# Layer one's kernel product in four row tiles over four banks, new places in its queue, and filler products at the end of retention

## The chip, the cores and the metric

One Trainium2 chip, one of its cores. The metric is the device time of one execution of the whole program in microseconds. Engines: TensorE (PE; PEld is its loading of weights), VectorE (DVE), ScalarE (ACT), GpSimd (POOL), and SyncE (SP), which issues DMAs.

## The reference, cut to what matters

Two layers on x of shape 16 x 1024 x 256. Layer zero is a retention block with an MLP, then a mixture of 16 experts with a top-k choice over all tokens. Layer one is a dynamic convolution with a softmax over 31 taps, then an MLP with a ReLU. The change touches the convolution's kernel and, in layer zero, only what TensorE does while the last tile of retention is normalised.

```python
# layer one, attention: b=16, l=1024, H=16 heads of d=16 channels, K=31 taps
avg = jnp.cumsum(x, axis=1) / jnp.arange(1, l + 1)[None, :, None]
ci = avg.reshape(b, l, H, d).transpose(0, 2, 1, 3).reshape(b * H, l, d)
pc = ci @ W_pe + b_pe                      # the kernel product, 62 columns a head
dyn, gate = pc[..., :K], pc[..., K:]
energy = stt + sigmoid(gate) * dyn         # tanh form: (1 + tanh(gate/2)) * dyn/2
w = softmax(energy, axis=-1)
out = sum over kk of w[:, :, kk:kk+1] * padded[:, kk:kk+l, :]
v = layernorm(out @ W_fc.T + residual) * gamma + beta
# layer one, MLP
h = relu(h4 @ W1 + b1);  y = h @ W2 + b2
```

## The kernel before, in words

All engines run the same list of steps, each its own part of each step, in order. Layer one works on one batch (1024 tokens) at a time, cut in eight chunks of 128 tokens and two halves of 512. The list is made by hand: each step has a place in slots, sixteen slots to a batch (`PLACES_D`; `STARTS_D` for batches 0 and 1), and `order_d` and `layer_one_tiles` sort all steps of all batches by place. Steps of neighbouring batches overlap: a place above 16 falls into the next batch's time. So a place says only what comes before what in each engine's queue; nothing waits for a time. Engines meet through semaphores.

The steps on TensorE in layer one: `turn_in` (eight transposes of 128x128), `kernel_product` (one a chunk), `window_turn` (two transposes), `convolve` (32 matmul records; eleven a batch, of 96 tokens), `mix` (one a chunk), `turn_mid` (eight transposes a half), `l1_expand` and `l1_contract` (eight of each a half, six and twelve matmuls). In one slot stand one `l1_expand` and one `l1_contract`.

PSUM has eight banks. Banks 6 and 7 hold the MLP's sums. `timed_banks` shares out banks 0 to 5 to the other steps in order of place, by a hold time in slots for each kind of step (`BANKS_D`). A bank that is used again is waited for with the semaphore of whoever read it last: a kernel product's banks with `gated_energy` (VectorE, L2318), a convolution's with `convT` (ScalarE, L2215), turn_mid's with `l1_h_full` (ScalarE, L2225), a mix's with `l1_u` (VectorE, L2351), an expansion's with `l1_hidden_low` (VectorE, L2380).

The kernel product of a chunk, before: the 256 channels are two blocks (j) of 128; each block is cut in two row halves of 64 partitions (r), four heads each. A bias product (L2424) of 64 rows and 496 columns opens one bank for each r, then for each j and r a product of 64 rows and 248 columns (L2429) is added. An fp32 matmul shows as two records, the bias (fp32r) as one. Then ScalarE takes the tanh of the gate half of both banks (L2187), VectorE makes the gated energy from the other half (L2318), GpSimd adds the energies of the reference (L2147), VectorE subtracts the maximum (L2324, L2326), ScalarE exponentiates, VectorE divides, SyncE writes the weights to a band in DRAM and loads it back for the convolution.

After retention's last tile the program goes on with the experts' choice: 32 rounds of a search, each a count on VectorE and ScalarE, summed by TensorE (L1703, L1705, L1707); between them stand `turn_logits` in rounds 1 to 4 (four transposes each) and from round 5 on three filler products of 128x256 (`keep_clock`, L1695). Ahead of it the last tile's transposes (L1050) and routing (L1057) wait for a chain of small VectorE, GpSimd and ScalarE instructions.

Of the kernel before, what the change touches and what calls it, by code (L numbers as in the profile page):

```python
# [22 lines left out]
P = 128  # L23
BANK = 512
# [12 lines left out]
    "tensor": ["mod_product0", "cols_turned0"] + [f"mod_product{n}" for n in range(1, 6)] + ["cols_turned1"]  # L37
    + [event for n in range(1, ROUNDS + 1) for event in (f"counted_all{n}", *([f"logits_turned{n - 1}"] if n <= 4 else []))] + ["limits_spread", "first_counted_all", "first_summed", "all_counted", "ties_summed", "rows_summed"]
# [329 lines left out]
def timed_banks(steps, wanted, of, paired=()):  # L368

    free, at = {bank: 0.0 for bank in of}, {}  # L370
# [564 lines left out]
def retention_tensor(K, t, t0, pe):  # L935
# [108 lines left out]
    for h in range(2):  # L1044
        pe.wait_ge(s("xn"), t.N + h)
        bank = take(t.bank["turn_out", i, h], "xnT", KD * i + h + 1)
# [6 lines left out]
    for h in range(2):  # L1053
# [5 lines left out]
        m.then_inc(s("lg_product"), 1)  # L1059

# [619 lines left out]
def expert_tensor(K, t, pe):  # L1680
# [16 lines left out]
    for n in range(1, ROUNDS + 1):  # L1697
# [121 lines left out]
    "l1_split": 0.6, "l1_low": 1.03, "l1_contract": 2.59, "share": (4.65, 12.15), "load": (0.54, 8.56), "join": (4.76, 13.01),  # L1819
    "add_in": (6.08, 13.95), "stats_in": (6.42, 14.39), "root_in": (7.3, 15.44), "norm_in": (7.84, 15.72), "load_bias_row": 4.42,  # L1820
    "turn_in": (9, 17.63), "average": (9.98, 10.16, 17.95, 18.16), "add_row": (11.69, 19.69),
    "kernel_product": (10.8, 12.8, 14.85, 16.8, 18.8, 20.8, 22.79, 24.8), "gated": (10.8, 12.8, 14.61, 16.8, 18.82, 20.8, 22.8, 24.8),
    "energies": (11.61, 13.56, 15.61, 17.61, 19.47, 21.61, 23.61, 24.94), "exponentials": (11.89, 13.82, 15.85, 17.92, 19.85, 21.85, 23.85, 25.7),
# [817 lines left out]
```

## Time and profile before

| | us |
|---|---|
| median of 3 runs | 3453.86 (3453.41 to 3455.07) |
| profiled execution | 3465.23 |
| its span | 3463.4 |
| TensorE busy in the span | 3306.8 (95%) |
| VectorE busy | 2606.7 (75%) |
| ScalarE busy | 2073.9 (60%) |
| GpSimd busy | 1256.2 (36%) |
| TensorE's mean granted clock | 0.978 |

The busy time is the share in which at least one instruction of the engine ran; matmuls overlap, and their ends are modelled. Retention takes the span to about 1070 us, the experts to about 1940, layer one the rest.

### The profile page before, as it was taken

The page shows a single profiled execution, that of the slowest core. Times are in us where ns is not written, and L with a number is a line of the kernel's source. Part 1 is how long each engine was busy: PE and PEld are TensorE (multiplying, and loading weights), DVE is VectorE, ACT ScalarE, POOL GpSimd, SP SyncE. Part 2 cuts the span into 40 slices and gives each one's busy share as a digit, 9 for nine tenths or more (in the row PEclk, how much of TensorE's full clock was granted, in tenths as well). Part 3 has the DMA queues.
Part 4 walks back from the last instruction along what each step waited for, and adds up shares of the span by engine and source line. Part 5 has one row for each costly group of instructions (what it writes and reads, how often), then busy time and mean ns, then how long its engine had stood idle before and what let it go on. Part 6 is the DMA issues. An engine that isn't in the chain of part 4 may idle for free.

```text
span 3463.4 us, 67571 instructions
## 1 busy us (share of the span) xinstructions
PE 3306.8 (95%) x25145; PEld 2791.9 (81%) x25145; DVE 2606.7 (75%) x6178; ACT 2073.9 (60%) x4056; POOL 1256.2 (36%) x1076
## 2 busy tenths in 40 slices
PE   7999999999997899999999469999999999999999
PEld 4888888888886789999999448888888888888888
DVE  5877887788878865555554588888888888888884
ACT  4677777777665455556665345555555555555554
POOL 1333323333322256656655332333333332322320
PEclk8999999999998999999999779999999999999999
DMA  5332233222212544444444365555555555655541
GB/s 180 102 115 99 84 114 108 82 66 76 75 45 80 93 103 106 95 106 106 107 95 91 84 132 117 117 121 126 129 125 127 121 123 126 130 126 127 128 102 41
DMA packets 746054, 366.38 MB, mean 106 GB/s; under 512 B 551311, under 2 KB 696279, under 8 KB 745591
## 3 DMA queue, kind: packets, MB, share of 16 engines
q1 hardware_dynamic: 717246, 319.55, 36.9%
q0 software_dynamic: 28416, 42.49, 6.9%
q8 instruction: 201, 3.29, 0.4%
q14 instruction: 127, 1.03, 0.1%
q10 hardware_dynamic: 64, 0.02, 0.0%
HBM read 224.93 MB, written 135.99 MB: 104 GB/s over the span
## 4 chain that ended last, share of the span: by engine, by line
PE 88%; DVE 6%; ACT 2%; issue 1%; DMA 1%; SPq 1%; POOL 1%; another core or an unknown queue 0%; ACTq 0%; DVEq 0%; POOLq 0%
PE bank L2479 11%; PE bank L2493 10%; PE bank L1015 10%; PE bank L1781 10%; PE bank L1797 10%; PE bank L994 10%; PE bank L2450 7%; PE bank L130 5%; PE bank L971 3%; PE bank L2429 3%; PE bank L2461 3%; PE bank L2424 1%; ACT sides L1327 1%; PE bank L979 1%; PE bank L1007 1%
## 5 line engine op out<-in xcount | busy, mean ns | idle before, releaser
L1670 DVE TENSOR_TENSOR hidden_low<-bank,hidden_high 128x512 fp32r<-128x512 f32 x256 | 176.2, 689 | 247.3 <-ACT hidden_high L1380 148.9
L641 ACT ACTIVATE bank<-bank,b 128x512 f32<-128x512 f32 x256 | 172.4, 673 | 281.5 <-PE bank L994 281.2
L1373 ACT ACTIVATE bank<-bank,fc_bias 128x512 f32<-128x512 f32 x256 | 169.6, 663 | 253.5 <-PE bank L1781 231.9
L1015 PE MATMUL bank<-w_high,gT_low 128*128 128x256 f32 x1024 | 309.6, 302 | 2.9 <-DVE gT_low L782 2.9
L2237 ACT ACTIVATE bank<-bank,l_b 128x512 f32<-128x512 f32 x256 | 168.8, 659 | 239.4 <-PE bank L2479 239.4
L2493 PE MATMUL bank<-l_w_high,l_hidden_low 128*128 128x256 f32 x1024 | 307.5, 300 | 0.0
L2450 PE MATMUL bank<-bandT,window 128*32 128x96 f32 x5632 | 272.7, 345 | 22.4 <-DMA bandT<-bands 18.9
L1015 PE MATMUL bank<-w_high,gT_high 128*128 128x256 f32 x1024 | 289.5, 283 | 0.0
L1015 PE MATMUL bank<-w_low,gT_high 128*128 128x256 f32 x1024 | 289.4, 283 | 0.0
L2493 PE MATMUL bank<-l_w_low,l_hidden_high 128*128 128x256 f32 x1024 | 285.9, 279 | 0.0
L2493 PE MATMUL bank<-l_w_high,l_hidden_high 128*128 128x256 f32 x1024 | 285.6, 279 | 0.0
L2450 PEld LDWEIGHTS bank<-bandT,window 128*32 128x32 f32 x5632 | 194.7, 123 | 84.7 <-issue 48.1
L782 DVE TENSOR_TENSOR gT_low<-bank,gT_high 128x512 fp32r<-128x512 f32 x256 | 173.0, 686 | 112.5 <-ACT gT_high L648 112.5
L2147 POOL TENSOR_TENSOR energies<-energies,energy 128x496 f32<-128x496 f32 x128 | 161.7, 1264 | 207.6 <-DVE energies L2318 207.6
L1293 POOL DMA_INDIRECT moe_output<-ys,idx x128 | 204.1, 1594 | 70.4 <-issue 55.1
L2479 PE MATMUL bank<-h4T_high,l_w_low 128*128 128x512 f32 x512 | 222.9, 435 | 6.7 <-DVE l_v L2351 6.7
L1015 PEld LDWEIGHTS bank<-w_high,gT_low 128*128 128x128 f32 x1024 | 195.1, 191 | 24.0 <-issue 13.1
L2493 PEld LDWEIGHTS bank<-l_w_high,l_hidden_low 128*128 128x128 f32 x1024 | 192.6, 188 | 23.4 <-issue 19.0
L994 PE MATMUL bank<-hT_high,w_low 128*128 128x512 f32 x512 | 203.7, 398 | 2.7 <-POOL hT_low L563 2.7
L1015 PEld LDWEIGHTS bank<-w_low,gT_high 128*128 128x128 f32 x1024 | 195.4, 191 | 12.0 <-issue 7.2
L994 PE MATMUL bank<-hT_low,w_high 128*128 128x512 f32 x512 | 203.4, 397 | 0.0
L2479 PE MATMUL bank<-h4T_high,l_w_high 128*128 128x512 f32 x512 | 202.8, 396 | 0.0
(400 smaller groups left out, 10703.7 us busy)
## 6 DMA issues: line engine op xcount, KB each, us to landing
bandT<-bands SPq DMA_DIRECT2D x352, 240.0 KB, 3.7
fc_full<-in_L_ffn_fc_wT SPq DMA_DIRECT2D x32, 1024.0 KB
bands<-zeros SPq DMA_DIRECT2D x22, 768.0 KB, 8.6
x<-in_L_attn_x SPq DMA_DIRECT2D x32, 512.0 KB, 6.3
moe_output<-zeros SPq DMA_DIRECT2D x32, 512.0 KB, 7.2
moe<-moe_output SPq DMA_DIRECT2D x32, 512.0 KB, 7.0
x_after_retention<-x SPq DMA_DIRECT2D x31, 512.0 KB, 2.8
moe_input_and_gates<-xn SPq DMA_DIRECT2D x31, 512.0 KB, 7.8
```

Of the source, the lines that this page charges most:

```text
L130: t = pe.transpose(bank[:, i * rows:(i + 1) * rows], source(i), ident[0:rows, 0:rows])
L641: e.activation(bank[:, :], bank[:, :], ACT.Gelu_apprx_tanh, bias=t.b1[:, f:f + 1]).then_inc(s("g_full"), 1)
L782: v.tensor_tensor(t.gT.low[:, f % SLICES, :], K.banks[t.bank["expand", i, f, 0]][:, :], t.gT.high[:, f % SLICES, :], ALU.subtract).then_in ...
L994: m = pe.matmul(bank[:, :], w, h, start=k + j == 0, stop=k == KD - 1 and j == 2)
L1015: m = pe.matmul(out, x, w, start=False, stop=f == KF - 1 and j == 2 and c % 2 == 1)
L1293: e.indirect_dma_start(K.moe_dram, bass.IndirectOffsetOnAxis(ap=t.idx[i % 4][:, n:n + 1], axis=0), t.ys[i % 2][:, n, :], None, compute_op= ...
L1670: v.tensor_tensor(t.hidden.low[:, n % SLICES, :], K.banks[t.bank["expand", i, f, 0]][:, :], t.hidden.high[:, n % SLICES, :], ALU.subtract) ...
L1781: m = pe.matmul(bank[:, :], w, y, start=k + j == 0, stop=k == KD - 1 and j == 2)
L1797: p = pe.matmul(y_chunk(K, ch), y, w, start=first and j == 0, stop=f == KF - 1 and j == 2 and ch % 2 == 1)
L2450: m = pe.matmul(bank[32 * g:32 * (g + 1), k * TT:(k + 1) * TT], t.window[n % 2][:, pair, odd, :], t.bandT[n % 2][:, :, g // 2 * H // 2 + k ...
L2479: m = pe.matmul(bank[:, :], w, x, start=k + j == 0, stop=k == KD - 1 and j == 2)
L2493: p = pe.matmul(K.banks[6 + ch // 2][:, left:left + D], x, w, start=False, stop=f == KF - 1 and j == 2 and ch % 2 == 1)
```

## The change

Layer one. The kernel product is cut in four row tiles of 32 partitions (two heads of each block), each into a bank of its own: four bias products of 248 columns, then for each block four products of 124 columns, where there were two of 496 and two of 248 for each block. The order of heads in the energies follows, and so do the constants made on the host, the loads (14 instead of 10) and the view that tanh and gated energy read (four banks of 124 elements, 496 in all as before). A kernel product takes the banks 0 to 3, all four; expansions take only 4 and 5; all other steps 0 to 3. All places are new.

Retention. Twenty-four filler products of 128x256 (fp32, so two records each) are put on TensorE between the last contraction of the last tile and its transposes, in groups of 5, 5, 6, 5 and 3, the later four each behind a wait. Three of the four `turn_logits` move from rounds 1 to 3 of the search to the end of retention, with five fillers behind them; the fourth moves to round 1, and rounds 2 to 4 get fillers.

```diff
 def timed_banks(steps, wanted, of, paired=(), homes={}):
+        home = homes.get(name, of)
         if name in paired:
-            first = min(of[::2], key=lambda b: max(free[b], free[b + 1]))
-            taken = [first, first + 1]
+            first = min(home[:len(home) - number + 1], key=lambda b: (max(free[b:b + number]), -sum(free[b:b + number])))
+            taken = list(range(first, first + number))
         else:
-            taken = sorted(of, key=lambda b: free[b])[:number]
+            taken = sorted(home, key=lambda b: free[b])[:number]
...
 def retention_tensor
+    halves = [take(t.bank["turn_out", i, h], "xnT", KD * i + h + 1) for h in range(2)]
+    def keep_clock(count):
+        for _ in range(count):
+            pe.matmul(halves[1][:, 0:D], K.ident[:, :], t.w_ret[:, 0, :], start=True, stop=True)
+    keep_clock(5)
+    for signal, value, count in (("x1", t.N, 5), ("x1", t.N + 1, 6), ("h2", t.N, 5), ("var_rms", t.N, 3)):
+        pe.wait_ge(s(signal), value)
+        keep_clock(count)
...
+    pe.wait_ge(s("centered"), t.N)
+    for n in range(3):
+        turn_columns(pe, K.banks[4 + n], C, lambda c: K.logits[:, (n * C + c) * P:(n * C + c + 1) * P], K.ident, s("tensor_setup"))
+    keep_clock(5)
...
 def expert_tensor
-        if n <= CH // PER_BANK:
-            turn_logits(n - 1)
+        if n == 1:
+            turn_logits(CH // PER_BANK - 1)
         else:
             keep_clock(3 if n < ROUNDS else 1, 2 * P)
...
-    "kernel_product": (10.8, 12.8, 14.85, 16.8, 18.8, 20.8, 22.79, 24.8),
+    "kernel_product": (11.07, 12.98, 14.92, 16.69, 18.96, 20.99, 22.77, 24.6),
-    "convolve": (16.82, 18.13, 19.59, 21.03, 22.48, 23.93, 25.38, 26.83, 28.28, 29.73, 31.18),
+    "convolve": (16.8, 18.08, 19.67, 21.36, 22.28, 23.89, 25.49, 26.84, 28.19, 29.73, 31.09),
-    "turn_mid": (29.71, 36.62),
+    "turn_mid": (30.8, 37.6),
...
 BANKS_D = {
-    "turn_in": (2, 0.44), "kernel_product": (2, 0.7), "window_turn": (1, 0.48), "convolve": (1, 0.45), "mix": (1, 0.61), "turn_mid": (2, 0.18),
-    "l1_expand": (1, 1.97),
+    "turn_in": (2, 0.77), "kernel_product": (4, 0.37), "window_turn": (1, 0.55), "convolve": (1, 0.46), "mix": (1, 2.41),
+    "turn_mid": (2, 1.48), "l1_expand": (1, 2.27),
 }
+HOMES_D = {name: range(4) for name in BANKS_D} | {"l1_expand": range(4, 6)}
...
-            for r in range(2):
-                rows = slice(r * P // 2, (r + 1) * P // 2)
-                pe.matmul(pair[r][:, 0:4 * t.RW], t.ones[rows, :], t.pe_bias[rows, :, :, :, :].rearrange("o a j q k -> o (a j q k)"), start=True, stop=False)
+            for r in range(t.NR):
+                rows = slice(r * P // t.NR, (r + 1) * P // t.NR)
+                pe.matmul(pair[r][:, 0:2 * KD * t.RW], t.ones[rows, :], t.pe_bias[rows, :, :, :, :].rearrange("o a j q k -> o (a j q k)"), start=True, stop=False)
             for j in range(KD):
-                for r in range(2):
-                    rows = slice(r * P // 2, (r + 1) * P // 2)
+                for r in range(t.NR):
+                    rows = slice(r * P // t.NR, (r + 1) * P // t.NR)
```

The expansion's place is unchanged, 33.2 and then every slot; the contraction's moves from 2.59 to 2.53 slots behind it. In the queue of a steady batch after the change, `window_turn` 10 stands at 30.54, a contraction at 30.73, `turn_mid` of half 0 at 30.8, the next batch's `kernel_product` 2 at 30.92 (14.92), `convolve` 10 at 31.09, `mix` 6 at 31.11, an expansion at 31.2.

## Rows read from the trace of the kernel before

**Rows 1.** The page, part 1: busy time, share of the span, instructions.
```profile
PE 3306.8 (95%) x25145; PEld 2791.9 (81%) x25145; DVE 2606.7 (75%) x6178; ACT 2073.9 (60%) x4056; POOL 1256.2 (36%) x1076
```

**Rows 2.** Windows: busy us of each engine, granted clock, DMA share, GB/s.
```profile
1080.00:1090.00 10.00, 8.84 (x33) 7.36 (x31) 7.68 (x25) 6.09 (x13) 0.00 (x0) 0.62 0.71 255
1090.00:1100.00 10.00, 8.53 (x45) 7.09 (x44) 9.82 (x32) 7.23 (x16) 1.04 (x1) 1.00 0.18 59
2480.00:2570.00 90.00, 89.52 (x828) 73.95 (x827) 77.91 (x159) 52.30 (x106) 27.44 (x22) 1.00 0.57 125
```

**Rows 3.** Waits from 2100 to 3400 us: total us, times, longest.
```profile
DVE top L2324 <- POOL energies L2147: 87.9, 84, 2.0
...
PE bank L2479 <- DVE l_v L2351: 6.7, 14, 0.5
```

**Rows 4.** Timeline of TensorE in two batches: start us, us, engine, line.
```profile
2479.99 0.49 PE L2424 MATMUL bank<-pe_bias,l_ones 64*128 64x496 f32 x2
...
2570.00 0.49 PE L2424 MATMUL bank<-pe_bias,l_ones 64*128 64x496 f32 x2
...
2602.86 0.49 PE L2424 MATMUL bank<-pe_bias,l_ones 64*128 64x496 f32 x2
2603.18 1.00 PE L2429 MATMUL bank<-w_pe,avgT 64*128 64x248 f32 x8
2604.11 1.56 PE L2450 MATMUL bank<-bandT,window 128*32 128x96 f32 x32
...
2607.32 1.04 PE L130 MATMUL bank<-ident,moe 128*128 128x128 f32 x8
```

**Rows 5.** Timeline around one kernel product with idle readers.
```profile
2491.97 0.49 PE L2424 MATMUL bank<-pe_bias,l_ones 64*128 64x496 f32 x2
...
2493.34 0.58 ACT L2187 ACTIVATE l_th<-bank 128x496 f32<-128x496 f32 x1 [0.20 <-PE bank L2429]
...
2493.96 0.67 DVE L2318 SCALAR_TENSOR_TENSOR energies<-l_th,bank 128x496 f32<-128x496 f32 x1 [0.34 <-ACT l_th L2187]
```

**Rows 6.** Timeline around one turn_mid.
```profile
2444.38 1.04 PE L130 MATMUL bank<-ident,l_v 128*128 128x128 f32 x8
...
2445.01 1.45 ACT L2225 ACTIVATE l_h_full<-bank,mod_columns 128x512 f32<-128x512 f32 x2 [0.65 <-PE bank L130]
2446.35 1.14 ACT L2231 CAST h4T_high<-l_h_full 128x512 fp32r<-128x512 f32 x2
```

**Rows 7.** Timeline around one convolution.
```profile
2609.69 1.50 PE L2450 MATMUL bank<-bandT,window 128*32 128x96 f32 x32
...
2611.11 0.50 PE L2479 MATMUL bank<-h4T_high,l_w_low 128*128 128x512 f32 x1
...
2611.25 0.32 ACT L2215 COPY convT<-bank 128x192 f32<-128x192 f32 x1 [0.65 <-PE bank L2450]
```

**Rows 8.** Timeline of TensorE at the end of retention and in the search.
```profile
1063.41 2.19 PE L1050 MATMUL bank<-ident,xn 128*128 128x128 f32 x8 [9.76 <-DVE xn L890]
...
1074.35 0.35 PE L1707 MATMUL bank<-count,ones_of_count 128*128 128x2 f32 x1
...
1087.71 0.25 PE L1707 MATMUL bank<-count,ones_of_count 128*128 128x2 f32 x1
...
1089.87 0.25 PE L1707 MATMUL bank<-count,ones_of_count 128*128 128x2 f32 x1
...
1089.98 1.54 PE L1695 MATMUL bank<-logits,block_ones 128*128 128x256 f32 x6
```

**Rows 9.** Timeline: an expansion, the draining of its bank, the next but one.
```profile
2572.72 0.50 PE L2479 MATMUL bank<-h4T_high,l_w_low 128*128 128x512 f32 x1
...
2574.22 0.38 PE L130 MATMUL bank<-ident,avgT 128*128 128x128 f32 x2
...
2582.93 0.67 DVE L2380 TENSOR_TENSOR l_hidden_low<-bank,l_hidden_high 128x512 fp32r<-128x512 f32 x1
...
2583.40 0.48 PE L2479 MATMUL bank<-h4T_high,l_w_low 128*128 128x512 f32 x1
```

More of the change, by code:

```diff
@@ L1043, in retention_tensor @@
     i, q = t.N - 1, P // C
-    for h in range(2):
+    halves = [take(t.bank["turn_out", i, h], "xnT", KD * i + h + 1) for h in range(2)]
[6 more added lines that the diff above has]
+        keep_clock(count)
+    for h, bank in enumerate(halves):
         pe.wait_ge(s("xn"), t.N + h)
-        bank = take(t.bank["turn_out", i, h], "xnT", KD * i + h + 1)
         for k in range(KD):
@@ L1818 @@
 PLACES_D = {
[L1819 to L1822, printed above, removed]
@@ new lines @@
+    "norm_in": (8.66, 14.98), "load_bias_row": 3.83, "turn_in": (9.17, 16.89), "average": (9.5, 9.63, 16.92, 18.28),
+    "add_row": (11.84, 19.96), "kernel_product": (11.07, 12.98, 14.92, 16.69, 18.96, 20.99, 22.77, 24.6),
+    "gated": (10.93, 12.74, 14.76, 16.64, 18.55, 20.58, 22.76, 24.59),
+    "energies": (11.31, 13.55, 15.76, 17.45, 19.29, 21.42, 23.52, 25.44),
+    "exponentials": (12.04, 14.05, 15.81, 18.0, 20.12, 22.01, 23.98, 25.68),
+    "softmax": (12.53, 14.65, 16.56, 18.43, 20.63, 22.63, 24.33, 26.31),
@@ L1830 @@
+    "turn_mid": (30.8, 37.6), "load_out_row": 38.29, "gain_out": (42.51, 50.94), "result": (47.78, 57.02),
 }
@@ L1945, in layer_one_tiles @@
     t.x2, t.moe = K.ring(ctx, "x2_", 2, [P, HC, D]) + more_x2, K.ring(ctx, "moe", 2, [P, HC, D])
-    t.loads = 16 * 10
+    t.loads = 16 * 14
     course = sorted(((2 * KF * b + place, n, name, b, *args) for b in range(K.B) for n, (place, name, *args) in enumerate(order_d(KF, b))), key=lambda z: z[:2])
     t.steps = [(name, b, *args) for _, _, name, b, *args in course]
-    t.bank = timed_banks([(time, *step) for time, _, *step in course], BANKS_D, range(6), ("kernel_product",))
+    t.bank = timed_banks([(time, *step) for time, _, *step in course], BANKS_D, range(6), ("kernel_product",), HOMES_D)
     t.pieces, t.w_count, sent = {}, {}, [0, 0]
@@ L1996, in layer_one_sync @@
     loads = [(t.out_full[0:2, :, :], A["L1_ffn_b2"].rearrange("(a b d) -> a b d", a=1, b=1).to_broadcast([2, 2, D]))]
-    loads += [(t.pe_full[r:r + 2, :, :, :, :].rearrange("o a j q k -> o (a j q k)"), A["pe_bias_row"].to_broadcast([2, 4 * t.RW])) for r in (0, P // 2)]
+    loads += [(t.pe_full[r:r + 2, :, :, :, :].rearrange("o a j q k -> o (a j q k)"), A["pe_bias_row"].to_broadcast([2, 2 * K.KD * t.RW])) for r in range(0, P, P // t.NR)]
     def load_half(b, half):
@@ L2249, in kernel_view @@
     first = t.bank["kernel_product", b, ch, 0]
-    assert t.bank["kernel_product", b, ch, 1] == first + 1
-    two = K.psum[:, first * BANK:(first + 2) * BANK].rearrange("p (r c) -> p r c", r=2)
-    return two[:, :, part * K.KD * t.RW:(part + 1) * K.KD * t.RW]
+    assert all(t.bank["kernel_product", b, ch, r] == first + r for r in range(t.NR))
+    tiles = K.psum[:, first * BANK:(first + t.NR) * BANK].rearrange("p (r c) -> p r c", r=t.NR)
+    return tiles[:, :, part * K.KD * t.RW:(part + 1) * K.KD * t.RW]
 def layer_one_vector(K, t, v, c):
```

110 lines of the change are left out of this document (58 added, 52 removed).

## The prediction, made before the changed kernel ran

> **What bounds the kernel now.** I read the page first: TensorE is busy for 3306.8 us, 95% of the span [rows 1]. That counts overlapping matmuls with modelled ends, so it names the engine and no more. The windows come next. A steady batch of layer one holds 89.52 us of TensorE work in 90 us at a granted clock of 1.00, against 77.9 us of VectorE, 52.3 of ScalarE and 27.4 of GpSimd [rows 2]. The first kernel product of one batch starts at 2479.99 and that of the next at 2570.00, so a batch takes 90.0 us [rows 4]. The view of waits between 2100 and 3400 us has one wait of TensorE, 14 times 0.48 us: an expansion whose bank VectorE hasn't yet drained of a mix [rows 3]. VectorE's own longest wait there is 87.9 us for GpSimd's sum of the energies [rows 3]. So in layer one TensorE's issue order is the path and the rest fits beneath it, VectorE with the least room (12 us in 90, much of it spent in waits). Fourteen batches, 2 to 15, run so. Batches 0 and 1 are a start-up paced by other engines and by DMA.
>
> The second place is the end of retention. The granted clock is 0.62 for 1080 to 1090 us and 1.00 in the ten after [rows 2], behind an idle stretch of 9.76 us in which TensorE waits for the last normalised tile [rows 8]. Those hundred microseconds are a chain through VectorE, ScalarE and TensorE, so the lost clock lies on the path.
>
> **Part A, TensorE kept busy at retention's end.** The count of a search round starts at 1074.35 (round 2), 1087.71 (round 7), 1089.87 (round 8): five rounds at the low clock took 13.36 us, one at the full clock 2.16 [rows 8]. At 2.16 the five take 10.8, which is 2.6 us less. Against it stand 24 added filler products of 128x256 ahead of the last tile, two records each. Six such records have their first start at 1089.98 and end 1.54 us later [rows 8], so with 0.28 for one record's run they start 0.25 apart at most; I take 0.22, 0.43 us a product and 10.4 us for 24. The last work before the idle stretch ends at 1053.65 (1063.41 less 9.76), so they run to about 1064, 0.6 us past the 1063.41 at which the first transposes start now; those then take half as long, and the second half waits for VectorE as before. After the routing, twelve transposes at 0.11 and five fillers come to 3.5 us. With the routing half as long they end near 1070.3. The next stage begins about then anyway: its second count is at 1074.35, its first a slow round earlier. If they are 1 us late, Part A is worth 1.6. I take **2.6 us**, between 0 (the clock isn't held) and 3.5 (round 1 and the routing gain too).
>
> **Part B, the kernel product.** Now two bias products of 496 columns, then eight records of 248 on 64 rows: 2602.86 to 2604.11, 1.25 us [rows 4]. The eight take 1.00 us from the first start to the last end; the two halves of the array run side by side (eight one after another at the 0.207 us that 496 column passes need at 2.4 GHz would take 1.66). So there are four steps of 0.207 us. The change makes four tiles of 32 rows: sixteen records of 124 columns, still four steps if four tiles run side by side. A step is then no longer set by its columns (0.103) but by loading 128 columns of weights: eight transposes with such loads and few columns take 1.04 us including one run of 0.27 [rows 4], so 0.11 us a step. The four steps fall from 0.83 to 0.44, the bias phase by half of 0.207. A product takes 0.75 us, **0.50 less; eight a batch, 4.0 us.** Tanh and the gated energy keep their 496 elements.
>
> The bounds: no gain would need the four tiles to run in pairs, 0 us. Between them lies what the convolution shows, the only tiles cut four ways in this trace: 32 records in 1.56 us with runs near 0.34 [rows 4], 0.157 us for a step of four tiles whose 192 column passes need 0.08. If row tiles keep such a step, four take 0.63 and the product 0.95: 2.4 us a batch. I take 0.11, since here, unlike in the convolution, the trace shows row tiles whose loads hide (eight records in 1.00 us).
>
> The Trainium skill, "TensorE: Matmul & The Clock Gate", section "Measured speedup vs the span model", has 3.07 times for four row tiles of 512 columns, not four. By that, as an estimate, a step of 0.11 becomes 0.14 us, the product gains 0.37 us, and the forecast would be some 15 us later. No run here shows it yet.
>
> **What the four banks cost.** Each kernel product now takes banks 0 to 3 at once. It can't start until all four are drained, and nothing but an expansion (banks 4, 5) or a contraction (6, 7) can run until VectorE has finished the gated energy. From an undisturbed product: start 2491.97, tanh 2493.34, gated 2493.96 to 2494.63 [rows 5]. The banks are free 2.66 us after the start, with the shorter product 2.16, so 1.4 after its end. An expansion or a contraction is about 1.5 us (expansion 2572.72, next step 2574.22 [rows 9]), which just covers it. Sorting the new places of a steady batch gives the queue. Products 3, 4, 5, 6, 7 have one such step behind them, products 0 and 1 two: covered. Product 2 has none: its places run turn_mid 14.80, kernel_product 14.92, convolve 15.09.
>
> - Product 2. turn_mid uses banks 2 and 3. In the trace its transposes start at 2444.38, ScalarE's copies at 2445.01 for 1.45, its casts at 2446.35 for 1.14 [rows 6]. Banks are free 2.1 us after the start, so the product starts there and not at 0.95; its tanh, third in ScalarE's queue, starts at about 3.0; tanh and gated energy end 1.3 us later; the convolution starts at 4.4. With no waits it would start at 1.75. **2.65 us** a batch.
> - Product 0 stands right behind a convolution. Convolution 2609.69, copy 2611.25 for 0.32, TensorE's next step now 2611.11 [rows 7]: **0.5 us**.
> - Products 3 and 7: an expansion is just ahead, so its ReLU is ahead of the tanh, and VectorE is short of time there by the sum of its instructions. I take **0.3 us each**, between nothing and one 0.67 us VectorE instruction.
>
> That is 3.75 us a batch. The wait of 0.48 us goes, as expansions have banks of their own. Net: 4.0 + 0.48 - 3.75 = 0.7 us a batch, **10 us** in fourteen. In batches 0 and 1 products wait for averages and bands; four small DMAs more at the start lie under the load that layer one waits for. I put both at nothing, give or take 4.
>
> The Trainium skill's page "TensorEngine Tiling (Array Packing)", sections "PSUM Bottleneck" and "Gotcha 1: PSUM Pressure", warns of just this: row tiles need a bank each, and draining doesn't get faster. The trace agrees that draining takes longer (1.4 us after the product) than the product itself (0.75).
>
> **Sum.** 10 + 2.6 = 12.6 us. The profiled execution took 3465.2 us (span 3463.4), 11 above the median of the runs, so I take off the difference only: 3453.9 - 12.6, about **3441 us**.
>
> **Rivals.**
> 1. *The order hides the waits.* If ScalarE reaches product 2's tanh early, or what waits there is made up by work TensorE would have lost elsewhere, most of the 4.5 us a batch stays: 14 x 4.5 + 2.6 = 66 us, 3388. For it: VectorE has 12 us spare, and other work now stands between gated and energies. Against it: both engines take steps in order, and turn_mid, tanh and gated energy are one chain.
> 2. *Small tiles don't overlap load and run.* Step 0.157 in place of 0.11: product 0.95, 1.6 us a batch lost, net -0.9: 14 x 0.9 - 2.6 = 10 us slower, 3464. It decides from a step of 0.13 us on. For it the convolution; against it the present row tiles.
> 3. *Two banks for expansions.* Now the expansion started at 2572.72 is drained when VectorE's instruction of 2582.93 ends, 10.9 us later, while the next but one starts at 2583.40 [rows 9]; with two banks it would wait 0.2 us, and TensorE is to be faster. If four of sixteen expansions wait 0.8 us, 3.2 a batch: 45 us lost, 3486. It decides from 0.7 us a batch. Against it: gated energies that must be done at once keep VectorE near TensorE.
> 4. *It washes out:* a microsecond a batch more of waits than I counted, 3450 to 3457.
>
> **Chances.** My sum 0.35, rival 1 0.25, rival 4 0.17, rival 2 0.11, rival 3 0.10, others 0.02. Within 0.2% (7 us) can't be told from no change in this kernel. Rival 1 and most of my case lie below 3447: faster 0.58; same 0.18; slower 0.24. The range for 8 in 10 is 3400 to 3474: it holds my case, 2 and 4 and the nearer part of 1; the far ends of 1 and 3 are left out. My case's own range is 3430 to 3450.
>
> **What would show it.** A kernel product's start to the next step's 0.75 us, and its four records at one time starting within nanoseconds; if it is 0.95, rival 2. The distance of batches 89.3; TensorE idle before the convolution behind product 2 with the gated energy named as releaser, near 2.6 us each time; if it is absent, rival 1. Waits of expansions for hidden_low: rival 3. At retention's end clock 1.00 from 1050 on and rounds of 2.16 from the first; if the clock falls all the same, Part A fails. The forecast is most easily wrong in product 2's wait and in what I left at nothing in batches 0 and 1.

## The result, and the profile after

Median of 13 runs 3463.24 us after, 3455.07 before (13 runs on the same chip). The ratio is 1.0022, 95% interval 1.0014 to 1.0030: 7.6 us slower (4.8 to 10.4). I had forecast 12.6 us faster. The time lies within the range that I gave, on the other side of no change. One of the 13 runs after took 5254 us at a mean granted clock of 0.56; the ratio leaves it out.

The two profiled executions differ by 0.8 us only (3465.2 and 3466.0; spans 3463.4 and 3464.2): that of before lay 10 above its median, that of after 3. The counts of the search end at 1158.47 before, and layer one's first tanh starts 803.5 us later; in the kernel with retention's edit alone, whose code between these points is the same, it is 794.8 us, and 791.7 in the profiled execution after. So that of before lost some ten microseconds there with the same code, and whole spans can't be compared here. Below I compare distances within a stage, and the timed runs.

The busy times of the page:

```profile
PE 3270.6 (94%) x26501; PEld 2773.9 (80%) x26501; DVE 2638.1 (76%) x6178; ACT 2084.1 (60%) x4056; POOL 1304.5 (38%) x1076
```

TensorE is busy 36 us less than in [rows 1], in 1356 more instructions; VectorE 31 us more. The windows (us, busy time of PE, PEld, DVE, ACT, POOL, granted clock, DMA share, GB/s):

```profile
1080.00:1090.00 10.00, 8.89 (x43) 7.31 (x42) 9.15 (x27) 7.71 (x17) 0.00 (x0) 0.93 0.64 241
...
2207.00:2297.00 90.00, 86.62 (x925) 71.93 (x917) 79.75 (x160) 53.13 (x106) 29.25 (x22) 1.00 0.61 126
2476.00:2566.00 90.00, 86.56 (x882) 71.88 (x882) 78.73 (x156) 52.93 (x106) 29.71 (x22) 0.98 0.59 124
```

At retention's end the clock is 0.93 where [rows 2] had 0.62. In layer one TensorE idles 3.4 us of 90, where it idled 0.5; and the third line has a clock of 0.98, where [rows 2] had 1.00 in a batch. The waits from 2100 to 3400 us (total us, times, longest):

```profile
PE bank L2476 <- DVE energies L2344: 21.1, 14, 1.6
...
PE bank L2450 <- ACT l_h_full L2251: 15.5, 13, 1.2
...
DVE top L2350 <- POOL energies L2173: 9.5, 16, 0.8
...
PE bank L2450 <- ACT convT L2241: 8.9, 14, 0.7
...
PEld bank L2505 <- DVE l_hidden_low L2406: 4.3, 14, 0.3
```

The one wait of TensorE in [rows 3] is gone, and three larger ones stand in its place: a convolution for a gated energy, a kernel product for turn_mid's copies, a kernel product for a convolution's copy. A timeline of TensorE, with five starts of batches and, at 2395.94, one product and the step behind it (start, duration, engine, line):

```profile
2206.62 0.39 PE L2450 MATMUL bank<-pe_bias,l_ones 32*128 32x248 f32 x4 [0.64 <-ACT convT L2241]
...
2296.28 0.39 PE L2450 MATMUL bank<-pe_bias,l_ones 32*128 32x248 f32 x4 [0.64 <-ACT convT L2241]
...
2395.94 0.39 PE L2450 MATMUL bank<-pe_bias,l_ones 32*128 32x248 f32 x4
2396.16 0.61 PE L2455 MATMUL bank<-w_pe,avgT 32*128 32x124 f32 x16
2396.70 0.50 PE L2505 MATMUL bank<-h4T_high,l_w_low 128*128 128x512 f32 x1
...
2658.17 0.39 PE L2450 MATMUL bank<-pe_bias,l_ones 32*128 32x248 f32 x4 [0.64 <-ACT convT L2241]
...
2749.33 0.39 PE L2450 MATMUL bank<-pe_bias,l_ones 32*128 32x248 f32 x4 [0.64 <-ACT convT L2241]
...
2839.10 0.39 PE L2450 MATMUL bank<-pe_bias,l_ones 32*128 32x248 f32 x4 [0.64 <-ACT convT L2241]
```

A product takes 0.76 us to the next step's start (1.25 in [rows 4]): as forecast. These batches take 89.66, 91.16 and 89.77 us. Of the thirteen from batch 2 (2115.49) to batch 15 (3292.11) six take 91.1 to 91.3, five 89.7 to 89.8, two 90.2 and 90.7; the last seven alternate. The mean is 90.51, where it was 90.0 and I had forecast 89.3. What makes a long one shows at product 2. All engines there:

```profile
2676.61 1.04 PE L130 MATMUL bank<-ident,l_v 128*128 128x128 f32 x8
...
2677.25 1.45 ACT L2251 ACTIVATE l_h_full<-bank,mod_columns 128x512 f32<-128x512 f32 x2 [0.65 <-PE bank L130]
...
2678.84 0.39 PE L2450 MATMUL bank<-pe_bias,l_ones 32*128 32x248 f32 x4 [1.19 <-ACT l_h_full L2251]
...
2679.73 0.58 ACT L2213 ACTIVATE l_th<-bank 128x496 f32<-128x496 f32 x1
...
2680.35 0.67 DVE L2344 SCALAR_TENSOR_TENSOR energies<-l_th,bank 128x496 f32<-128x496 f32 x1 [1.72 <-ACT l_th L2213]
2680.93 2.35 DVE L2401 TENSOR_TENSOR h4T_low<-l_h_full,h4T_high 128x512 fp32r<-128x512 f32 x2
2681.09 1.64 POOL L2173 TENSOR_TENSOR energies<-energies,energy 128x496 f32<-128x496 f32 x1 [3.51 <-DVE energies L2344]
...
2681.16 1.50 PE L2476 MATMUL bank<-bandT,window 128*32 128x96 f32 x32 [1.50 <-DVE energies L2344]
```

From transposes to product 2.23 us, from product to convolution 2.32, as worked out (2.1 and 2.3). What I had left out comes behind it. The windows of 1 us there, with the clock as the third number from the end:

```profile
2680.00:2681.00 1.00, 0.00 (x0) 0.00 (x0) 0.65 (x2) 1.00 (x3) 0.00 (x0) 1.00 0.80 86
...
2682.00:2683.00 1.00, 1.00 (x19) 0.71 (x11) 1.00 (x1) 0.54 (x2) 0.74 (x1) 0.58 0.79 81
2683.00:2684.00 1.00, 1.00 (x5) 0.81 (x4) 0.89 (x2) 0.00 (x0) 0.00 (x0) 0.50 0.37 50
2684.00:2685.00 1.00, 1.00 (x4) 0.81 (x3) 0.00 (x0) 0.00 (x0) 0.00 (x0) 0.50 0.29 91
2685.00:2686.00 1.00, 1.00 (x4) 0.79 (x4) 0.90 (x3) 0.00 (x0) 0.00 (x0) 0.71 0.55 167
```

After the two idle stretches of 1.19 and 1.50 us the granted clock goes from 1.00 (2.4 GHz) to 0.50 (1.2 GHz) for 3 us, while a mix and an expansion run. The batches of 91.2 us have this, those of 89.7 don't, though they have the same two waits: it happens eight times in the fourteen steady batches. In the batch that starts at 2568.0 the low clock fell in part on the idle stretch itself, and the batch took 90.2.

Retention's end:

```profile
1067.00 1.10 PE L1060 MATMUL bank<-ident,xn 128*128 128x128 f32 x8
...
1074.38 0.27 PE L1724 MATMUL bank<-count,ones_of_count 128*128 128x2 f32 x1 [0.46 <-DVE hits L1461]
...
1088.41 0.25 PE L1724 MATMUL bank<-count,ones_of_count 128*128 128x2 f32 x1
```

The eight transposes take 1.10 us, not the 2.19 of [rows 8]. These counts are of rounds 1 and 7: six rounds in 14.03 us, while before rounds 2 to 7 alone, five, took 13.36 [rows 8]. The last tile came 3 us later in this execution than in that of before, ahead of anything changed. From retention's last product with both high halves (L1016) to the last count of the search it is 104.5 us after (1054.02 to 1158.53), and 107.4 before (1051.06 to 1158.47).

### The profile page after: what moved, and what is told of

Read it like the earlier page. It is cut to its first block, busy times and chain, and to the rows that moved or that the text cites. A ratio compares the mean times of both kernels' runs of the same rounds, so it can differ in the third digit from the quotient of the medians.

```text
span 3464.2 us, 70416 instructions
## 1 busy us (share of the span) xinstructions
PE 3270.6 (94%) x26501; PEld 2773.9 (80%) x26501; DVE 2638.1 (76%) x6178; ACT 2084.1 (60%) x4056; POOL 1304.5 (38%) x1076
## 4 chain that ended last, share of the span: by engine, by line
PE 88%; DVE 4%; ACT 3%; issue 2%; DMA 1%; POOL 1%; SPq 1%; PEldq 0%; PEld 0%; ACTq 0%; POOLq 0%; DVEq 0%
PE bank L2505 11%; PE bank L2519 11%; PE bank L1016 10%; PE bank L1814 10%; PE bank L1798 10%; PE bank L995 10%; PE bank L2476 7%; PE bank L130 6%; PE bank L2487 3%; PE bank L972 3%; PE bank L2455 1%; PE bank L2450 1%; PE bank L2485 1%; ACT sides L1344 1%; PE bank L980 1%
## 5 line engine op out<-in xcount | busy, mean ns | idle before, releaser
L2173 POOL TENSOR_TENSOR energies<-energies,energy 128x496 f32<-128x496 f32 x128 | 195.2, 1525 | 742.1 <-DVE energies L2344 742.1
L1016 PE MATMUL bank<-w_high,gT_low 128*128 128x256 f32 x1024 | 309.6, 302 | 2.9 <-DVE gT_low L783 2.9
L2476 PE MATMUL bank<-bandT,window 128*32 128x96 f32 x5632 | 264.0, 340 | 36.8 <-DVE energies L2344 27.1
L1016 PE MATMUL bank<-w_high,gT_high 128*128 128x256 f32 x1024 | 289.5, 283 | 0.0
L1016 PE MATMUL bank<-w_low,gT_high 128*128 128x256 f32 x1024 | 289.4, 283 | 0.0
L2476 PEld LDWEIGHTS bank<-bandT,window 128*32 128x32 f32 x5632 | 188.1, 123 | 91.5 <-issue 64.4
L1310 POOL DMA_INDIRECT moe_output<-ys,idx x128 | 212.2, 1658 | 70.4 <-issue 55.1
L2505 PE MATMUL bank<-h4T_high,l_w_low 128*128 128x512 f32 x512 | 230.2, 450 | 0.1
L1016 PEld LDWEIGHTS bank<-w_high,gT_low 128*128 128x128 f32 x1024 | 195.1, 191 | 24.0 <-issue 13.1
L1016 PEld LDWEIGHTS bank<-w_low,gT_high 128*128 128x128 f32 x1024 | 195.4, 191 | 12.0 <-issue 7.2
L2505 PE MATMUL bank<-h4T_low,l_w_high 128*128 128x512 f32 x512 | 203.1, 397 | 0.0
```

What stands on the lines that cost most here:

```text
L1016: m = pe.matmul(out, x, w, start=False, stop=f == KF - 1 and j == 2 and c % 2 == 1)
L1310: e.indirect_dma_start(K.moe_dram, bass.IndirectOffsetOnAxis(ap=t.idx[i % 4][:, n:n + 1], axis=0), t.ys[i % 2][:, n, :], None, compute_op= ...
L2173: e.tensor_tensor(e1[:, :, :], e1[:, :, :], t.energy[:, :, :], ALU.add).then_inc(s("full_energy"), 1)
L2476: m = pe.matmul(bank[32 * g:32 * (g + 1), k * TT:(k + 1) * TT], t.window[n % 2][:, pair, odd, :], t.bandT[n % 2][:, :, g * H // t.NR + k * ...
L2505: m = pe.matmul(bank[:, :], w, x, start=k + j == 0, stop=k == KD - 1 and j == 2)
```

## The experiments

**Theory 1:** layer one's steady batches lose the time, by the waits at product 2 and the clock that falls behind them. **Theory 2:** the loss comes from the edit at retention's end. **Theory 3:** VectorE is so full that a wait taken away comes back elsewhere. Theory 4 came up on the way. All kernels were timed against the kernel before on the same chip; the times below are the ratio less one times 3455 us, with the 95% interval. Edits of places are to the steady batches' table alone.

### One part at a time

Retention's end alone: the kernel before with these edits of the change, `keep_clock` groups, `turn_logits` and all.

```diff
+    keep_clock(5)
+    for signal, value, count in (("x1", t.N, 5), ("x1", t.N + 1, 6), ("h2", t.N, 5), ("var_rms", t.N, 3)):
...
-        if n <= CH // PER_BANK:
-            turn_logits(n - 1)
+        if n == 1:
+            turn_logits(CH // PER_BANK - 1)
```

> The kernel before with the edit at retention's end alone (filler products, early turning of three groups of logits); layer one as before. Theory 1 (the loss of 8 us comes from layer one's steady batches: TensorE waits 1.2 us ahead of and 1.5 us behind kernel product 2, and in every second batch the granted clock then falls to one half for some 3 us, 1.5 us more): 2.2 us faster than before, by the lead that the changed kernel's count of round 7 has gained on that of before since the last tile's store of it began. Theory 2 (the loss comes from the edit at retention's end, whose fillers and turned logits delay something that the profile of one execution hides): 3 us or more slower than before.

**Measured:** 5.2 us faster (1.7 to 8.3 faster). The stretch from the last high product to the last count is 105.0 us (107.4 before).

Layer one alone: the changed kernel with these edits taken back.

> The changed kernel with retention's end as before; layer one as changed. Theory 1: the changed kernel's time plus 2.2 us, so 10 us slower than the kernel before. Theory 2: at most the time of the kernel before.

**Measured:** 11.1 us slower than before (7.9 to 14.5); that stretch is 107.6 us. Theory 2 falls. Retention's end brings 2.4 to 3.1 us in the profiles; the timed runs (5.2, and 11.1 less 7.6) agree within their intervals. The loss is in layer one.

### The clock

Filler products in the two waits around product 2, so that these stay and TensorE works in them; four and six, then two and three.

```diff
+            if ch == 2 and b >= 2:
+                for _ in range(4):
+                    pe.matmul(pair[0][:, 0:D], K.ident[:, :], t.w_fc[:, 0, :], start=True, stop=True)
...
+                for _ in range(6):
+                    pe.matmul(K.banks[bank][:, 0:D], K.ident[:, :], t.w_fc[:, 0, :], start=True, stop=True)
```

> The changed kernel with filler products on TensorE in the two waits around product 2, in batches 2 to 15: four products of 128x256 into the product's first bank ahead of it, six into the next expansion's bank behind it. The waits stay, the engine works in them. Theory 1: granted clock 1.00 in all steady batches, which all take 89.7 us in place of 89.7 and 91.2 in turn, so some 10 us less than the changed kernel (3453). If the clock has no part in the loss: the same time as the changed kernel, or up to 3 us more for fillers that run over.

**Measured:** 23.2 us slower than before (18.3 to 27.6). The clock was 1.00 in all steady batches, but they took 91.4 us: the four fillers took 1.8 us and the six 2.8, longer than the waits. The number of fillers was wrong.

> As the run with filler products in the two waits around product 2, but two ahead and three behind in place of four and six. In that run each filler took 0.46 us in place of the 0.22 reckoned with, four took 1.8 us in a wait of 1.2 and six 2.8 in one of 1.5; the granted clock was 1.00 throughout, and batches took 91.4 us, 1.8 more than the 89.6 of the changed kernel's batches at full clock. Theory 1: clock 1.00 in all steady batches, all of 89.7 us, 10 us less than the changed kernel, so within 3 us of before. If the batches of 91.2 had another cause than the clock: 90.5 on average as in the changed kernel.

**Measured:** 0.3 us slower than before (2.8 faster to 3.5 slower), 7.3 less than the changed kernel. A batch, and two starts 89.65 apart:

```profile
2570.00:2660.00 90.00, 88.97 (x918) 73.34 (x916) 80.34 (x159) 52.95 (x106) 30.11 (x23) 1.00 0.59 125
```

```profile
2206.40 0.39 PE L2454 MATMUL bank<-pe_bias,l_ones 32*128 32x248 f32 x4 [0.64 <-ACT convT L2241]
...
2296.05 0.39 PE L2454 MATMUL bank<-pe_bias,l_ones 32*128 32x248 f32 x4 [0.64 <-ACT convT L2241]
```

All batches but the first of the thirteen (91.5) take 89.6 to 89.8, and the clock is 1.00 in all. TensorE does more work in the same waits and the kernel gets faster. The low clock costs 1.4 us each time that it comes.

### Moving product 2

```diff
-    "kernel_product": (11.07, 12.98, 14.92,   "gated": (10.93, 12.74, 14.76,
+    "kernel_product": (11.07, 12.98, 15.22,   "gated": (10.93, 12.74, 15.27,
-    "convolve": (... 31.09),  "mix": (... 31.11, 32.15),  "center_mid": (... 31.31, 32.31)
+    "convolve": (... 31.75),  "mix": (... 31.77, 32.15),  "center_mid": (... 31.8, 32.31)
```

> The changed kernel with kernel product 2 of the steady batches placed behind the expansion at 15.20 in place of ahead of it, its convolution 10 and mix 6 behind the contraction at 15.73, gated energy 2 and the sixth subtraction moved likewise. The expansion now covers turn_mid's copies and the contraction covers tanh and gated energy. Theory 1: the waits of 1.2 and 1.5 us go, and the clock stays at 1.00: 2.7 us a batch and 0.8 on average for the clock, 13 batches, 45 us less than the changed kernel (some 37 less than before), batches of 87.0 us. Theory 3 (VectorE's queue is the limit, so that a wait taken away at product 2 comes back elsewhere, as waits of expansions for hidden_low or of convolutions for the gated energy): less than 15 us below the changed kernel, batches of 89 us or more.

**Measured:** 14.2 us slower than before (9.3 to 18.7). The convolution still waits:

```profile
2680.83 2.09 ACT L2193 ACTIVATE moe<-more_x,l_center_in,l_root_in 128x256 f32<-128x256 f32 x4
...
2683.38 0.57 ACT L2213 ACTIVATE l_th<-bank 128x496 f32<-128x496 f32 x1
...
2683.99 0.67 DVE L2344 SCALAR_TENSOR_TENSOR energies<-l_th,bank 128x496 f32<-128x496 f32 x1 [1.64 <-ACT l_th L2213]
...
2684.81 0.51 PE L2476 MATMUL bank<-bandT,window 128*32 128x96 f32 x8 [2.18 <-DVE energies L2344]
```

The product's last tile had started before 2681.0. ScalarE was in norm_in (L2193), whose place 14.98 the tanh had been moved past. A moved step is moved past the others' steps on each engine that has a part in it. Behind this single wait of 2.18 us the clock fell too, to 0.50 from 2686 to 2689, and so in seven batches. With norm_in behind the tanh:

```diff
-    "norm_in": (8.66, 14.98)
+    "norm_in": (8.66, 15.3)
```

> As the run that moved kernel product 2 behind the expansion, with ScalarE's four norm_in products moved behind that product's tanh as well (14.98 to 15.30). In the first run of this kind they stood ahead of the tanh: product 2 ended at 2681.0, ScalarE was on norm_in until 2682.9, then on a ReLU until 2683.5, the tanh came at 2683.38, the gated energy ended at 2684.66 and the convolution started at 2684.81, behind a contraction that had ended at 2682.6. Theory 1 (the waits at product 2 and the clock are the loss, and a queue of ScalarE held them up there): tanh right behind the ReLU at about 2681.6, the convolution's wait 0.3 us in place of 2.2, clock 1.00, batches of 87 to 88 us; 25 to 40 us less than the changed kernel, so 15 to 35 us less than before. Theory 3 (VectorE's queue is the limit): a wait of like size appears elsewhere and batches stay above 89 us.

**Measured:** 9.7 us faster than before (5.9 to 13.1), 17 us less than the changed kernel. Clock 1.00; two starts of batches 88.77 apart, and the waits:

```profile
2562.78 0.39 PE L2450 MATMUL bank<-pe_bias,l_ones 32*128 32x248 f32 x4 [0.64 <-ACT convT L2241]
...
2651.55 0.39 PE L2450 MATMUL bank<-pe_bias,l_ones 32*128 32x248 f32 x4 [0.67 <-ACT convT L2241]
```

```profile
PE bank L2450 <- DVE l_v L2377: 14.9, 13, 1.2
...
PE bank L2476 <- DVE energies L2344: 8.4, 14, 1.6
```

Theory 1 has the direction, not the size: 1.5 us a batch in the mean of thirteen (89.05 against 90.51) where 2.5 to 3.5 were expected, because a new wait of 1.1 us came (product 3, for a mix's bank) and 0.6 stayed at the convolution.

### The waits that are left

Product 0 behind an expansion too:

```diff
-    "kernel_product": (11.07,   "gated": (10.93,
+    "kernel_product": (11.22,   "gated": (11.27,
```

> As the run beside it, and kernel product 0 of the steady batches moved behind the expansion at 11.20 too (11.07 to 11.22), its gated energy from 10.93 to 11.27. Theory 1: the 0.64 us that product 0 waits for the convolution's copy goes, so 8 us less than the run beside it. Theory 3: no difference, or slower, as a gated energy stands behind one more VectorE instruction.

**Measured:** 32.5 us slower than before (27 to 38). The gated energy, now behind statistics and a draining on VectorE, starts 1.7 us after its tanh has ended; a mix waits for its bank, 1.1 us at first and 3.2 from 2660 us on, where the clock is 0.97 to 0.98.

VectorE's step result behind the two subtractions, and on top of it convolution 7 ahead of a contraction:

```diff
-    "result": (47.78,
+    "result": (48.45,
```

> As the run with product 2 and norm_in moved (batches of 88.8 us, 9 us less than before), and VectorE's step result of the first half moved from 15.78 to 16.45, behind the two subtractions of mixes 6 and 7. There kernel product 3 waited 1.14 us in every batch for the seventh of these subtractions, ahead of which stood result's 1.22 us on VectorE. Theory 1 (each wait is made by one step of another queue, and goes with its order): no wait of product 3, batches of 87.7 us, some 15 us less than the run before it, 24 less than the kernel before. Theory 3 (VectorE is so full that the wait moves on): batches of 88.5 or more.

**Measured:** 6.2 us faster than before (3.1 to 9.3), so 3.5 more than without this edit, within the intervals. The wait moved on:

```profile
PE bank L2476 <- DVE energies L2344: 22.3, 26, 1.6
...
PE bank L2450 <- DVE l_v L2377: 4.4, 13, 0.4
```

Product 3's wait is 10.5 us shorter, the convolutions' 13.9 longer.

```diff
-    "convolve": (... 25.49, 26.84, 28.19,
+    "convolve": (... 25.49, 26.72, 28.19,
```

> As the run beside it, and convolution 7 of the steady batches placed ahead of the contraction at 10.73 (10.84 to 10.72), so that kernel product 0 stands behind a contraction and not behind the convolution whose bank ScalarE is still copying. Product 0 waited 0.64 us for that copy in every batch. Theory 1: batches of 87.0 us, 9 us less than the run beside it. Theory 3: no difference.

**Measured:** 2.8 us slower than before (0.3 faster to 5.9 slower). Product 0 doesn't wait any more, but:

```profile
2923.58 1.29 DVE L2415 TENSOR_TENSOR o<-bank,row_out 128x512 f32<-128x512 f32 x2 [0.95 <-PE bank L2519]
2924.38 0.59 ACT L2213 ACTIVATE l_th<-bank 128x496 f32<-128x496 f32 x1 [1.58 <-PE bank L2455]
2924.79 1.66 DVE L2387 SCALAR_TENSOR_TENSOR more_x<-l_v,l_root_mid,more_x 128x256 f32<-128x256 f32 x4
2926.37 0.66 DVE L2344 SCALAR_TENSOR_TENSOR energies<-l_th,bank 128x496 f32<-128x496 f32 x1
```

gain_out (L2415) waits for the contraction that was moved behind the convolution, and with residual_mid (L2387) holds the gated energy 1.4 us. Both moved behind it, on the order of the 9.7 us with convolution 7 moved as above and result where it was:

```diff
-    "gain_out": (42.51,   "residual_mid": (26.7,
+    "gain_out": (42.95,   "residual_mid": (26.97,
```

> The fastest order so far (product 2 and norm_in moved, batches of 88.8 us, 9 us less than before) with convolution 7 ahead of the contraction as well, so that product 0 doesn't wait 0.64 us for the convolution's copy. In the run that did this first, VectorE reached gated energy 0 late: tanh ended at 2924.97, but gain_out waited for the delayed contraction, gain_out and residual_mid held VectorE until 2926.4, the gated energy ended at 2927.03 and a mix waited 1.3 us for its bank. Here gain_out (42.51 to 42.95) and residual_mid (26.7 to 26.97) of the first half stand behind that gated energy (10.93). Theory 1 (each wait comes from one step's place in a queue and can be ordered away): no wait of product 0 nor of the mix, batches of 88.1 us, 9 us less than the fastest order. Theory 3 (VectorE is so full in these stretches that one of its steps is late whichever comes last): the contraction's bias product, or the next expansion, waits for VectorE instead, and batches stay at 88.8 or more.

**Measured:** 41.8 us slower than before (36 to 47). Expansions wait for their bank's draining. Timeline of the place:

```profile
2854.67 1.28 DVE L2415 TENSOR_TENSOR o<-bank,row_out 128x512 f32<-128x512 f32 x2
...
2854.83 1.24 POOL L2173 TENSOR_TENSOR energies<-energies,energy 128x496 f32<-128x496 f32 x1 [11.11 <-DVE energies L2344]
...
2855.86 3.82 DVE L2387 SCALAR_TENSOR_TENSOR more_x<-l_v,l_root_mid,more_x 128x256 f32<-128x256 f32 x4
...
2856.03 2.58 POOL L2154 TENSOR_TENSOR more_x<-more_x,row_bias 128x1024 f32<-128x1024 f32 x1
...
2862.46 0.50 PE L2505 MATMUL bank<-h4T_high,l_w_low 128*128 128x512 f32 x1 [2.81 <-DVE l_hidden_low L2406]
```

The same four residual products that took 1.66 us take 3.82 beside GpSimd's sums; the expansion waits 2.81 us for a VectorE step behind them, and 2.2 of these are the stretch (3.82 less 1.66). The clock falls behind this wait too. So a **theory 4:** VectorE loses its room where an instruction of two SBUF inputs stands beside a GpSimd instruction, as GpSimd's sum of the energies always starts right behind a gated energy. Residual_mid was put back, gain_out alone left behind the gated energy (`"gain_out": (42.95,`):

> The run with convolution 7, gain_out and residual_mid moved came out 42 us slower than before: expansions waited 2.8 us in every batch. In its rows residual_mid's four products (1.66 us elsewhere) took 3.82 us behind the gated energy, since they ran beside GpSimd's sum of the energies (2854.83 for 1.24) and its row_bias sum (2856.03 for 2.58). Here residual_mid stays ahead of the gated energy (26.7) and gain_out alone (42.95) stands behind it: it reads a bank and one tile, and in that run took its usual 1.28 us beside GpSimd. Theory 4 (VectorE's room is lost where an instruction with two SBUF inputs stands beside a GpSimd instruction): no stretch, no wait of expansions, batches of 88.1 us, 9 us less than the fastest order so far. Theory 3 (VectorE is simply full there): the wait comes back in another place, batches of 88.8 or more.

**Measured:** 9.0 us faster than before (5.2 to 12.4), 51 us less than with residual_mid moved. That step's group in both, busy us and mean ns of one from 2200 to 3280 us, first the slow kernel, then this one:

```profile
L2387 DVE SCALAR_TENSOR_TENSOR more_x<-l_v,l_root_mid,more_x 128x256 f32<-128x256 f32 x72 | 59.4, 883 | 0.0
```

```profile
L2387 DVE SCALAR_TENSOR_TENSOR more_x<-l_v,l_root_mid,more_x 128x256 f32<-128x256 f32 x72 | 39.1, 604 | 0.0
```

The expansions' waits are gone with the stretch. Four steady batches take 89.6 us, then from batch 8 on 88.5; the former have a bias product waiting 1.1 us for gain_out. What changes at batch 8 isn't known. Product 0's wait is gone, batches of 88.1 didn't come, and nothing came of it in total. One more, on the order of the 9.7 us:

```diff
-    "result": (47.78,
+    "result": (49.3,
```

> The fastest order so far (batches of 88.8 us), with VectorE's step result of the first half moved from 15.78 to 17.3, behind gated energy 3 and an expansion's draining, and not to 16.45, where it took the 0.87 us from product 3's wait and gave 1.1 us to convolutions 10 and 0, as its 1.22 us stood right ahead of gated energy 3. Theory 1 and theory 4 alike: product 3 waits 0.3 us in place of 1.14 and convolution 0 not at all, batches of 88.0 us, 11 us less. Theory 3: batches of 88.8 or more.

**Measured:** 10.0 us faster than before (5.9 to 14.2). Product 3's wait falls by 10.5 us and products wait 7.3 us for an average instead. With the edits of both:

> The two edits of the runs beside it together. Theories 1 and 4: batches of 87.3 us, 20 us less than the fastest order so far, 29 less than before. Theory 3: no better than the better of the two.

**Measured:** 9.3 us faster than before (5.5 to 12.8). Four orders end within a microsecond of each other, and their intervals can't tell them apart. Theories 1 and 4 said 20 us less for this one; theory 3 said no better, which is what came. It doesn't show theory 3's reason: VectorE is busy 77.8 us a batch here and 78.9 in the order of the 9.7 us, so it gained a microsecond of room and the kernel nothing.

### The product in its old form

The changed kernel with two tiles of 64 rows in two banks, in its own order, then in that of the run with convolution 7 moved.

> The changed kernel (new places, expansions in banks 4 and 5, retention's end as changed) with the kernel product in its old form, two tiles of 64 rows in two banks. Convolution 10 then has a free bank and doesn't wait for the gated energy; product 2 still waits for turn_mid's copies. If the short product is worth its 0.5 us each on TensorE, as theory 1 says: 4.0 us a batch more for products, 1.5 and 0.6 less for the waits of convolution 10 and product 0, full clock, so batches of 91.6 us, 15 us over the changed kernel. If TensorE's time there isn't the path (theory 3): batches of 90 us or less, the same as the changed kernel or faster.

**Measured:** 11.1 us slower than before (6.9 to 15.5), 3.5 more than the changed kernel. The waits:

```profile
PE bank L2449 <- ACT l_h_full L2250: 14.3, 12, 1.2
```

Product 2 waits for turn_mid's copies all the same; the convolution and product 0 hardly ever wait, and the clock stays at 1.00: this one wait of 1.2 us didn't take it down. Batches take 90.8 us. I had expected 15 us over the changed kernel and not 3.5, which is within the intervals. Of the 4.0 us a batch that four tiles save on the products, this order gives back 2.1 in the waits of the convolution and product 0, 0.7 by the clock and some 0.8 in other steps; what is left is the 0.5 by which its batches are the shorter ones (90.51 and 90.99 in the mean).

> The order of the run beside it (product 2, norm_in, result and convolution 7 moved) with the kernel product in its old form, two tiles of 64 rows in two banks. If the four tiles are worth what the steps show (0.50 us a product, less about 0.8 a batch by which contractions, and steps right behind a product, take longer with four tiles), batches of 90.2 us, 40 us more than the run beside it and about as before. If the order alone brought the gain: within 5 us of the run beside it.

**Measured:** 19.7 us slower than before (14.9 to 24.5), 17 more than the same order with four tiles, where I had expected 40. The order alone brings nothing.

## Why the prediction was wrong

**Retention's end.** Right. Forecast 2.6 us, 2.4 to 3.1 in the profiles, 5.2 and 3.5 in the timed runs with wide intervals. Rounds of 2.16 us come from round 4 on and not from the first: rounds 1 to 3 took 2.3 to 2.6 us, in windows with clocks of 0.90 and 0.93.

**The product.** Right in mechanism and size: 0.50 us less, four records side by side. Rival 2 falls. The Trainium skill's 3.07 times in "TensorE: Matmul & The Clock Gate", "Measured speedup vs the span model", is for tiles of 512 columns; carried over to this product it gave, as an estimate, a gain of 0.37, and the trace has 0.50 for tiles of 124 and 248 columns.

**The waits at products 2 and 0.** Right: 1.19 and 1.50 against 2.65, 0.64 against 0.5. Products 3 and 7, forecast at 0.3 each, wait for nothing. The weight loads of expansions wait 0.3 us a batch for hidden_low; rival 3, with 3.2, didn't come. So the waits were 3.3 us a batch where I had 3.75. One reading of the prediction is wrong and changes nothing: the 87.9 us that it calls VectorE's longest wait is the sum of 84 waits, of which the longest is 2.0 us [rows 3].

**What failed in the steady batch: the waits were priced at their length.** I had weighed the clock at retention's end and not here. With idle stretches of 1.2 and 1.5 us around product 2 it fell to one half in eight of fourteen batches; 1.4 us each time, 7 to 10 us in all, is the largest missing term (shown by the fillers: 7.3 us). Without it a batch takes 89.65 where I said 89.3, though the waits were 0.4 shorter than forecast, so some 0.8 us is left. Of this, some steps right behind a product take longer than with two tiles (an expansion ahead of a window_turn 1.58 and 1.50, a contraction ahead of a convolution 1.76 and 1.60; an expansion ahead of a convolution 1.60 both times), and contractions ahead of a product 0.02 (1.52 and 1.50 us); for that I have no cause and made no test. In thirteen steady batches the change costs 0.47 us each, 6.1 us, where I had 0.7 gained.

**What failed besides: batches 0 and 1 at nothing, give or take 4.** From the first tanh to that of batch 2 it is 158.8 us before and 159.5 in the kernel with retention's edit alone (1952.61 to 2112.08). After, it is 166.1 (1950.25 to 2116.38); in three runs with the same code up to there it is 163.6 and 168.3 (fillers) and 164.2 (layer one alone). So this stretch differs by up to 4.7 us between executions of the same code, and the change costs 4 to 9 us in it, 6.4 in the mean of these. With two tiles in the new order it is 162.2 and 159.2, so a part seems to go with the four banks: in this stretch products waited up to 7.4 us for the gated energy of the one before. How the loss divides between the banks and the new order can't be told from single traces with that scatter; the start's order was not tried by itself.

**Sum.** Forecast 10 gained in layer one, found 11.1 lost: about 16 of the 21 us in steady batches, 6 to 7 in the start, less 1 in the last batch. Rival 1's mechanism (ScalarE early, waits made up elsewhere) is absent. Rival 4, a microsecond a batch more of waits, gives batches of 90.3 us and comes nearest to the 90.5, without what the start lost.

**Is the cause the waits at product 2?** Yes, with the clock that fell behind them, for the loss against before: with these ordered away the kernel is 9.7 us faster than before. But not for all that the product promises, 56 us in 14 batches. Everything further that was moved gave back what it took. That VectorE is stretched beside GpSimd (below) made the slowest order slow, but isn't what is left in the best ones: VectorE is busy 77.8 to 78.9 us a batch there and 77.9 before. What may be left are the four banks themselves: a product holds them until VectorE has made the gated energy, so VectorE must be on time eight times a batch with all it has to do. That this sets the end at 3445 is argued from four orders that end there, not shown.

## What to carry to other kernels

A shorter instruction on the bound engine is worth only as much as the engines that release its resources can follow. A product that takes all banks of a group is as long as the whole chain to the last reader of these banks, and here the waits around it also cost the clock. When a step is moved, list for every engine that has a part in it what it is moved past: four instructions of norm_in turned a gain of 10 us into a loss of 14. And look at what GpSimd does while a VectorE step runs: the same four instructions took 1.66 us and 3.82.

## What the runs showed of the hardware that I had not expected

**The clock falls in a stream that is 96% busy.** 2.7 us of idle time, with a product of 0.8 us between, was followed by a granted clock of 0.50 for 3 us, in eight of fourteen otherwise equal batches. With fillers in the same gaps it was 1.00 throughout. It was 1.00 as well with two tiles, where the wait of 1.2 us stands alone, while behind a single wait of 2.18 us it fell in seven batches.

**VectorE stands still beside GpSimd, for some instructions.** In the timeline of product 2 above, the two instructions for h4T_low take 2.35 us: the second starts at 2681.54, GpSimd's sum runs from 2681.09 to 2682.73, and the second ends at 2683.28. GpSimd's sum is longer there too, 1.64 us where it takes 1.24 undisturbed. With product 2 moved, all 48 of them take 0.69 us in the mean, where in the changed kernel it is 0.95. The order of the changed kernel has such places also at residual_mid (0.61 us each, 0.48 before); VectorE is busy 1.8 us a batch longer than in [rows 2] with the same instructions. The order of before has such places as well: its subtraction of the maximum takes 0.96 us in the mean (2.16 at 2487.94, where GpSimd's row_bias sum runs from 2487.15 for 2.42) and after the change 0.67. So the new order moved these places about more than it made them. The Trainium skill's page "SBUF — State Buffer", section "SBUF: two separate sides", says that a VectorE instruction with two SBUF inputs and a GpSimd instruction that reads SBUF share one pair of ports under a lock, and that the second to start is blocked until the first ends. By that rule the trace agrees: the instructions for h4T_low and the residual products, two SBUF inputs, are held; gain_out, with one input from a bank, takes its usual 1.28 us beside the same sum. But two inputs aren't needed: l_less_mean_x, of 128x4 with one, took 1.92 us at 2480.64, beside a row_bias sum that runs from 2480.18 for 2.36, and takes 0.17 elsewhere.

**Tiles of 32 rows overlap fully at small sizes.** Sixteen records of 124 columns take 0.61 us from the first start to the last end, with 0.11 us from one step of four to the next: the time that I had taken from transposes with full weight loads.
